# Graph layer on one core: the conversion of positions to row numbers moves to ScalarE, and GpSimd's quads follow TensorE's ranking by four

## The reference, cut to what matters

```python
h = relu(layernorm(x))                                   # 12500 x 256
in_deg  = min(segment_sum(1, dst), 511)
out_deg = min(segment_sum(1, src), 511)
sum3d   = segment_sum(edge_attr @ W_sum + b_sum, src)    # 212500 x 128 -> 12500 x 256
out = x + h + z_in[in_deg] + z_out[out_deg] + sigmoid(cent @ W_cent + b_cent) \
        + sigmoid(vor @ W_vor + b_vor) + sum3d
```

## Time and profile before

| | us |
|---|---|
| median of three runs | 2481.67 |
| the profiled execution's own time | 2482.59 |
| its span | 2480.7 |
| TensorE / VectorE / ScalarE / GpSimd busy | 1577.1 / 1687.3 / 815.4 / 1851.6 |
| first and last scatter (line 529) start | 22.1 and 2134.3 |

### The profile page before, as it was taken

How to read it: one execution, slowest core, us unless ns; L and a number is a source line. 1 busy time by engine, 2 the same in 40 slices (tenths; PEclk the granted TensorE clock), 3 DMA queues, 4 the chain that set the end, 5 groups by cost and what they waited for, 6 DMA issues and landing times.

```text
span 2480.7 us, 40112 instructions
## 1 busy us (share of the span) xinstructions
PE 1577.1 (64%) x8689; PEld 1170.5 (47%) x8689; DVE 1687.3 (68%) x5737; ACT 815.4 (33%) x4073; POOL 1851.6 (75%) x1869
## 2 busy tenths in 40 slices
PE   5756666766767432228766766555677776687776
PEld 1234544544545210016555555444566664566665
DVE  7867678888878621549888755444676665797767
ACT  3423322334333432534433332322233233001323
POOL 5777777777777777777777777777777777766776
PEclk7858766667775555558898887767799888898889
DMA  4356544445555553348777676666688777798997
GB/s 135 103 153 192 151 134 132 134 137 161 155 155 152 156 175 106 101 125 233 210 209 213 205 213 187 190 184 182 207 252 244 234 226 216 189 245 204 245 248 194
DMA packets 485070, 451.89 MB, mean 182 GB/s; under 512 B 72407, under 2 KB 444637, under 8 KB 484828
## 3 DMA queue, kind: packets, MB, share of 16 engines
q1 hardware_dynamic: 402782, 300.08, 45.0%
q0 software_dynamic: 78752, 136.44, 17.6%
q10 hardware_dynamic: 3294, 12.80, 1.6%
HBM read 319.28 MB, written 129.59 MB: 181 GB/s over the span
## 4 chain that ended last, share of the span: by engine, by line
POOL 23%; DMA 13%; issue 10%; DVE 5%; PE 3%; DVEq 1%; SPq 1%; ACT 0%; POOLq 0%; ACTq 0%
POOL sorted L529 22%; DMA edge_ring<-in_L_gnn_z_out_dram,out_i 4%; DMA piece_ring<-sorted 4%; DMA sorted<-edge_ring,pos_i 3%; DMA edge_ring<-in_edge_attr_dram 2%; PE bank L1019 2%; DVE acc L713 2%; DVE hot_n L686 1%; POOL edge_ring L546 1%; DVE gate_normed L752 0%; DVE base L801 0%; DVEq L713 0%; SPq L424 0%; PE bank L1038 0%; DVEq L401 0%
## 5 line engine op out<-in xcount | busy, mean ns | idle before, releaser
L529 POOL DMA_INDIRECT sorted<-edge_ring,pos_i x1660 | 1604.6, 967 | 527.5 <-issue 480.2
L1019 PE MATMUL bank<-piece_ring,hot_n 128*125 128x129 f32 x4920 | 866.1, 328 | 204.5 <-DVE hot_n L686 179.3
L1019 PEld LDWEIGHTS bank<-piece_ring,hot_n 128*125 128x125 f32 x4920 | 773.2, 227 | 346.5 <-DVE hot_n L686 305.0
L686 DVE SCALAR_TENSOR_TENSOR hot_n<-bank,wkey,piece_ring 128x250 f32<-128x250 f32 x1230 | 580.3, 472 | 478.0 <-DMA piece_ring<-sorted 453.9
L880 ACT ACTIVATE junk<-bank,mark_col 128x100 bf16<-128x100 f32 x1664 | 547.9, 340 | 180.9 <-PE bank L996 179.3
L1002 PE MATMUL bank<-hot_w,after_b 128*128 128x400 bf16 x416 | 177.7, 427 | 574.2 <-ACT junk L880 573.7
L887 ACT ACTIVATE edge_ring<-key_f 128x5 f32<-128x5 f32 x332 | 70.4, 212 | 1146.0 <-DMA edge_ring<-in_edge_attr_dram 1145.4
L713 DVE TENSOR_TENSOR acc<-bank,acc 125x129 f32 x1230 | 349.4, 284 | 41.5 <-issue 26.9
L1002 PEld LDWEIGHTS bank<-hot_w,after_b 128*128 128x128 bf16 x416 | 46.1, 111 | 643.9 <-ACT junk L880 643.8
L880 ACT ACTIVATION_READ_ACCUMULATOR junk<-bank,mark_col 128x1 f32 x1664 | 335.9, 202 | 0.0
L1045 PE MATMUL bank<-hot_dl,hot_dh 128*125 128x100 bf16 x1661 | 201.6, 277 | 30.0 <-DVE hot_dh L621 27.5
(11 more groups left out here) (109 smaller groups left out, 1145.3 us busy)
## 6 DMA issues: line engine op xcount, KB each, us to landing
piece_ring<-sorted SPq DMA_DIRECT2D x1230, 130.0 KB
edge_ring<-in_edge_attr_dram SPq DMA_DIRECT2D x332, 320.0 KB
sorted<-edge_ring,pos_i POOLq DMA_INDIRECT x1660
base<-in_x_dram SPq DMA_DIRECT2D x20, 560.0 KB
out_dram<-base ACTq DMA_DIRECT2D x19, 560.0 KB
out_dram<-base SPq DMA_DIRECT2D x9, 560.0 KB
base<-out_dram SPq DMA_DIRECT2D x9, 560.0 KB
edge_ring<-in_L_gnn_z_out_dram,out_i POOLq DMA_INDIRECT x100, 6.9
```

The source lines that it names most:

```text
L529: g.indirect_dma_start(rows, bass.IndirectOffsetOnAxis(index, 0), edge_ring[:, slot, at, :], None).then_inc(s_scatter[slot], 16)
L686: v.scalar_tensor_tensor(out=hot_n[:, n % HOT_SLOTS, 0:G, :], in0=iota_ps.unsqueeze(1).to_broadcast([P, G, LOC]), scalar=wkey[:, s % 2, c: ...
L1019: last = t_.matmul(to, hot_n[:, n % HOT_SLOTS, k, :], piece_ring[:, n % PIECE_SLOTS, k, 0:SUM], start=(k == 0), stop=(k == ROW_GROUPS[s] - 1))
```

## The change

`index(q)` goes from VectorE's loop to ScalarE's, right behind `positions(q)`, as an ACTIVATE of Copy instead of a CAST; `positions(q)` waits for `s_index` to reach q. GpSimd, from quad 8 on, additionally waits until `s_rank` has reached q+4 (416 at most), that is, until the quad q+3, counted from 0, has been ranked.

```diff
-INDEX_FIRST = 2
+RANK_LEAD = 4
@@ gpsimd
             for q in range(NQ):
                 pool.wait_ge(s_index, q + 1)
+                if q >= 2 * RANK_LEAD:
+                    pool.wait_ge(s_rank, min(q + RANK_LEAD, NQ))
                 for t in tiles(q):
@@ vector
-            def index(q):
-                dve.wait_ge(s_pos, q + 1)
-                if q >= INDEX_RING:
-                    c0 = (q - INDEX_RING) * QUAD
-                    for load in sorted({c // LOAD_TILES for c in range(c0, c0 + QUAD)}):
-                        dve.wait_ge(s_scatter[load % EDGE_SLOTS], 16 * LOAD_TILES * (load // EDGE_SLOTS + 1))
-                v.tensor_copy(pos_i[:, q % INDEX_RING, :], pos_f[:, q % 4, :]).then_inc(s_index, 1)
@@ vector, the loop
-                if q < INDEX_FIRST:
-                    index(q)
-                if q == NQ - 1:
-                    index(q - 1)
-                    index(q)
...
-                if INDEX_FIRST <= q - 1 < NQ - 2:
-                    index(q - 1)
@@ scalar
             def positions(q):
                 act.wait_ge(s_rank, q + 1)
-                if q >= 4:
-                    act.wait_ge(s_index, q - 3)
-                act.wait_ge(s_pos, q)
+                if q >= 1:
+                    act.wait_ge(s_index, q)
...
+            def index(q):
+                act.wait_ge(s_pos, q + 1)
+                if q >= INDEX_RING:
+                    c0 = (q - INDEX_RING) * QUAD
+                    for load in sorted({c // LOAD_TILES for c in range(c0, c0 + QUAD)}):
+                        act.wait_ge(s_scatter[load % EDGE_SLOTS], 16 * LOAD_TILES * (load // EDGE_SLOTS + 1))
+                a.activation(pos_i[:, q % INDEX_RING, :], pos_f[:, q % 4, :], ACT.Copy).then_inc(s_index, 1)
@@ scalar, the loop
                 positions(q)
+                index(q)
```

## The result

| | before | after |
|---|---|---|
| median of 13 runs each, us | 2481.45 (2477.43 to 2484.17) | 2488.53 (2485.61 to 2491.46) |
| profiled execution: time / span, us | 2482.59 / 2480.7 | 2491.46 / 2489.6 |
| last scatter starts (edge_last's, behind line 529's), us | 2135.6 | 2147.1 |
| from there to the end of the span, us | 345.1 | 342.5 |

The ratio is 1.0032, interval 1.0025 to 1.004: the change costs 7.1 us by the medians, where 9.2 had been forecast. In the profiled executions the sort ends 11.5 us later and the tail is 2.6 us shorter, together 8.9 us.

A forecast was written before the change was run, and what follows sets the result against it. GpSimd's scatters, running flat out, were taken to bound the kernel until the sort ends. Four stalls, 1.0 + 1.7 + 5.5 + 1.0 = 9.2 us, on the profiled 2482.6 gave 2491.8, as a median 2490.9 us; range 2484 to 2499.

The forecast's parts named there:

- Early waits go: GpSimd's waits of 0.85 and 2.45 us for indices 3 and 4 at the start vanish, gaining 2.7 us.
- Quad 8: GpSimd, arriving at 64.7 us, waits for rank 12; scatter 33 starts 1.0 us later than before, using up the 2.7.
- the earlier rank: Rank 12, needed at quad 8, comes 0.4 us earlier because five CASTs at 0.08 us leave VectorE.
- Quad 29: Early in the second segment, GpSimd waits for rank 33 before scatter 117: +1.7 us.
- Quad 214: Early in the third segment, GpSimd waits for rank 218 before scatter 857: +5.5 us.
- Quad 344: Early in the fourth segment, GpSimd waits for rank 348 before scatter 1377: +1.0 us.
- Waking: Where TensorE is late, GpSimd's scatter was taken to start 0.3 us after the rank ends.
- The tail: The time from GpSimd's last scatter to the end was to stay at 346 us; another length would count against the prediction.
- faster scatters: Rival: without VectorE's CASTs GpSimd's scatters lose all 15 us of excess, net -6 us, 2476 us; chance 0.05.
- The price on every quad: Rival: GpSimd's new wait costs time on every quad, 23 + 9.2 us, 2514 us; chance 0.04.
- The lead lost for long: Rival: delayed edge loads delay the ranks, so quads 215 to 219 stall anew, 7 us more, 2498 us; chance 0.08.
- the waits hardly bite: Rival: freed VectorE brings ranks 2 us or more earlier at each boundary; +3.5 us in all, 2485 us; chance 0.17.

## Why the prediction was right

The mechanism stood: GpSimd waits in the four places named and nowhere else, at 66, 177, 1126 and 1788 us. By its steps, with the shift of the same scatter against the kernel before:

- *Early waits go.* 2.7 us forecast; the shift at quad 4 is -2.4, and without the wait nothing replaces it. Right.
- *Quad 8.* +1.0 forecast, -0.8 measured (67.36 to 66.53), and the wait is 1.89 us long where 3.8 had been named. The step that failed is the earlier rank, 0.4 us from five CASTs at 0.08: rank 12 ended 2.8 us earlier (65.74 for 68.56). It is the index's move that does it: rank 12 ends at 65.26 with the index alone and at 68.50 with the wait alone. I had priced the CASTs and not what VectorE waited in front of them. In the kernel before its timeline reads:

```profile
21.64 0.17 DVE L815 CAST pos_i<-pos_f 128x4 int32<-128x4 f32 x1 [2.65 <-ACT junk L880]
...
24.33 0.18 DVE L815 CAST pos_i<-pos_f 128x4 int32<-128x4 f32 x1 [2.25 <-ACT junk L880]
24.68 0.53 DVE L599 TENSOR_SCALAR base<-base 128x732 f32<-128x732 int32 x1
```

In the kernel after, the same key work starts five microseconds earlier, with no wait in front:

```profile
18.53 1.18 DVE L623 TENSOR_TENSOR hot_w<-src_w,bank 128x400 bf16<-128x400 bf16 x4
19.63 0.53 DVE L601 TENSOR_SCALAR base<-base 128x732 f32<-128x732 int32 x1
```

- *Quad 29.* +1.7 forecast, +2.2 measured (the shift goes from -0.8 to +1.3).
- *Quad 214.* +5.5 forecast, +6.2 measured. Rank 218, which it needs, moved by 3.7 us, just what GpSimd's scatters had shifted by then. That is the reason given for adding the terms.
- *Quad 344.* +1.0 forecast, +3.0 measured; the gap is 3.3 us here and 4.7 in the change run again. Its rank moved by 9.9 us where GpSimd had shifted by 8.5, so it came 1.4 later than assumed. Of these, 1.2 lie between the end of rank 347 and the start of rank 348, where TensorE makes the list of pieces and the first piece products. Before, and then after (stretch, length, busy times as in the earlier trace rows, clock 0.65 and 0.53, means over a stretch in which the clock is now at 2.4 and now at 1.2 GHz):

```profile
1767.85:1777.47 9.62, 6.59 (x31) 5.25 (x32) 6.89 (x23) 1.62 (x9) 7.18 (x9) 0.65 0.58 177
...
1776.54:1787.39 10.85, 7.76 (x32) 6.00 (x31) 7.52 (x23) 1.72 (x10) 6.71 (x7) 0.53 0.54 173
```

  TensorE's work there took 1.17 us more at the lower granted clock; one product of the list, for instance, took 1.20 us for 0.69, where the granted clock was 0.74 (1775 to 1779 us) for 0.93 (1766 to 1770). It isn't the change that does it: the stretch is 10.9 us long with the index alone (clock 0.53), 10.8 with the wait alone (0.56), 11.0 in the change run again (0.55), and 9.6 with five quads of lead (0.64).
- *Waking.* In each of the four, 0.3 us had been taken from rank to scatter, and 0.78 was measured, 1.9 us in all. The 0.3 was read from scatters that carry their own wait. The second wait is a semaphore instruction of its own on GpSimd's sequencer, and its row in the trace after is

```profile
L522 POOLq EVENT_SEMAPHORE  x326: 17/17/17, 65.8 to 2126.6; - x163
```

with 0.73 us from its end to the scatter in all four. When it has not to wait it costs nothing (the equal gaps of 0.305 us), and in the swapped kernel, where the ranking's wait stands first, it is 0.28 us from rank to scatter.
- *Long scatters.* Between the stalls the shift drifts by +2.3 us (quads 30 to 213) and -1.3 (214 to 343). The gaps add up to the same within 0.02 us in both stretches, so it is all in the scatters' own time: those over 1 us fall elsewhere. No term had been set for it. The sum of -0.8, 2.2, 2.3, 6.2, -1.3 and 3.0 is, but for rounding, the 11.5 us of the last scatter (9.2 forecast).
- *The tail.* Forecast unchanged; 2.6 us shorter, and it is 341 to 343 us in the changed kernel and in all four of chip B, those without the wait or without the index included. The odd one is the 345 of the kernel before. Its second profile was taken on chip C, so whether 345 is chance is open. The prediction named a tail of another length as a sign of being wrong, and this part of it did fail. The sort lost 2.3 us more than forecast, and the shorter tail hides it: that the time came out within 2.4 us of the forecast is partly luck.

The rivals: faster scatters are refuted. The mean is 966 and 967 ns without the CASTs, and in the kernel before 369 scatters had one of these CASTs beside them and took 966 ns in the mean, the others 967. Of the scatters over 1 us, 69 of 74 before and 77 of 78 after ran beside a float operation of 256 or more columns on VectorE. The price on every quad is refuted by the equal gaps. The lead lost for long did not happen: quads 215 to 219 run without a gap, and ranks 219 to 224 moved by 3.5 to 3.9 us where GpSimd had moved by 9.8, so they do not follow it. Nor does it happen with five, where GpSimd had shifted by 22 us and rank 224 by 10.5; the stalls at 212 and 213 there are those that the late ranks 217 and 218 of the kernel before give. That the waits hardly bite was wrong at the three boundaries and right at the start, where VectorE was freed by more than the 2 us it named. The 2.4 us by which rank 12 came earlier than I had allowed about cancel the 1.9 of waking that I had missed, and that is luck too.

## What to carry to other kernels

When a stage is the bound, asking it to wait for a stage that feeds it bought nothing where the signals came on time (chip B), and gained where they came late (A and C). Count the lead at every boundary, because a lead of six in mid-segment hides the places where it is under four. When an instruction leaves an engine, take out with it what the engine waited in front of it. And run the two halves of such a change apart on more than one chip: here the index alone gains 0.25% and the wait loses 0.57% on one chip, while the same wait gains 4% on another.

## What the runs showed of the hardware

- A second semaphore wait in front of an indirect DMA on GpSimd costs nothing when it is satisfied (gaps of 304.8 ns for 304.9), and 0.5 us more than the other (0.78 for 0.28) when it is the last to be fulfilled. The wait written first goes with the DMA; the one written second becomes an instruction of its own.
- The stretch between two rankings in which TensorE makes the list of pieces of the fourth segment took 9.6 us at a granted clock of 0.64 or 0.65 and 10.8 to 11.0 at 0.53 to 0.56, in six traces of five kernels. Where GpSimd waits for the ranking, it waited for the end of this stretch.
- Scatters that took over 1 us in place of 0.96 ran beside float operations of 256 or more columns on VectorE (77 of 78 after); with a CAST of 4 columns beside it a scatter took 966 ns in the mean, without 967.
- Copy of 128x4 from float to int32 on ScalarE took 0.205 us, against 0.187 for VectorE's CAST.
- Two of the three chips of the experiments ran this one-core kernel 22 and 24% slower, with a read of ScalarE that began 11 us after the ranking it needed and GpSimd's scatters at their usual 0.96 us.
